# Experts ordered by the picks of eight sequences, and six expert groups taken ahead of the plan

## What is computed

```python
router_probs = softmax(flat_x @ router_w)            # 4096 tokens, 8 experts
topk_w, topk_idx = top_k(router_probs, 2)
topk_w = topk_w / sum(topk_w)
combine = sum(one_hot(topk_idx, 8) * topk_w[..., None], axis=1)
for e in range(8):
    h = gelu(flat_x @ w_fc[e])                       # 256 x 1024
    out = out + combine[:, e:e+1] * (h @ w_proj[e])  # 1024 x 256
```

## Time and profile before

| what | value |
|---|---|
| median of 3 runs | 686.19 us (685.14 to 688.24) |
| the profiled execution | 685.08 us |
| its span in the profile | 682.7 us, mean granted clock 0.961 |
| TensorE matmul busy | 615.7 us (90%) |
| VectorE busy | 490.1 us (72%) |
| GpSimd busy | 404.6 us (59%) |
| ScalarE busy | 397.0 us (58%) |

### The profile page before, as it was taken

The page is one execution under the profiler, slowest core; times in us unless marked ns, Lnnn a source line. Parts: engine busy times, 40 slices in busy tenths (PEclk is TensorE's granted clock), DMA queues, the critical chain, the costliest instruction groups (busy, mean ns, idle before and its releaser), DMA issues. The chain is left out here.

```text
span 682.7 us, 15315 instructions
## 1 busy us (share of the span) xinstructions
PE 615.7 (90%) x4664; PEld 587.4 (86%) x4664; DVE 490.1 (72%) x1162; ACT 397.0 (58%) x694; POOL 404.6 (59%) x298
## 2 busy tenths in 40 slices
PE   2796999999820999999999999999999999999993
PEld 2685888888720999999999999999999999999993
DVE  7663668788777687786768778676877868766661
ACT  3704666776524465656666565666656566656661
POOL 5101121667877567676676667667666766777773
PEclk9996999999965899999999999999999999999997
DMA  8906741232338446523131322313132232312111
GB/s 345 308 2 246 262 162 39 82 110 105 136 110 220 97 142 180 149 57 47 31 63 31 57 37 46 48 31 63 31 56 38 46 48 32 56 24 41 32 25 16
DMA packets 37588, 62.35 MB, mean 91 GB/s; under 512 B 3696, under 2 KB 32944, under 8 KB 36400
## 3 DMA queue, kind: packets, MB, share of 16 engines
q0 software_dynamic: 13296, 18.00, 14.8%
q1 hardware_dynamic: 14816, 34.56, 14.5%
q10 hardware_dynamic: 9440, 9.36, 5.5%
HBM read 37.02 MB, written 24.89 MB: 91 GB/s over the span
## 5 line engine op out<-in xcount | busy, mean ns | idle before, releaser
L625 POOL TENSOR_TENSOR pj_lo<-w_ffn,pj_hi 128x1024 fp32r<-128x1024 f32 x78 | 189.0, 2429 | 101.5 <-ACT pj_hi L685 96.8
L1368 DVE TENSOR_TENSOR fc_lo<-w_ffn,fc_hi 128x1024 fp32r<-128x1024 f32 x78 | 113.4, 1487 | 79.1 <-ACT fc_hi L685 79.1
L614 POOL DMA_INDIRECT out<-y,add_id x71 | 112.7, 1587 | 42.5 <-issue 41.5
L685 ACT ACTIVATE pj_hi<-w_ffn 128x1024 fp32r x78 | 82.6, 1060 | 89.7 <-PE psO L1693 77.0
L685 ACT ACTIVATE fc_hi<-w_ffn 128x1024 fp32r x78 | 79.0, 1053 | 36.5 <-issue 35.9
L1693 PE MATMUL psP<-pj_hi,h_hi 128*128 128x256 f32 x312 | 92.2, 295 | 2.7 <-DVE h_lo L1368 2.7
L1693 PE MATMUL psP<-pj_hi,h_lo 128*128 128x256 f32 x312 | 88.5, 284 | 0.0
L1693 PE MATMUL psP<-pj_lo,h_hi 128*128 128x256 f32 x312 | 88.3, 283 | 0.0
L582 POOL DMA_INDIRECT slots<-rows,slot x64 | 64.1, 1001 | 18.3 <-issue 16.5
L572 POOL TENSOR_TENSOR roots<-ve,power 128x6 f32<-128x6 f32 (+2 forms) x20 | 23.0, 1152 | 86.6 <-DVE ve L1045 85.6
L1693 PE MATMUL psO<-pj_lo,h_hi 128*128 128x256 f32 x256 | 72.6, 283 | 0.0
(11 more groups left out here) (302 smaller groups left out, 1592.0 us busy)
## 6 DMA issues: line engine op xcount, KB each, us to landing
w_ffn<-in_w_ffn SPq DMA_DIRECT2D x8, 2048.0 KB, 7.8
xg<-slots ACTq DMA_DIRECT2D x31, 265.0 KB, 2.9
xc<-in_x_ch SPq DMA_DIRECT2D x4, 1024.0 KB, 8.5
out<-x SPq DMA_DIRECT2D x16, 256.0 KB, 2.2
...
out<-y,add_id POOLq DMA_INDIRECT x71, 3.9
...
```

The lines of the kernel that those rows point to most:

```text
L614: nc.gpsimd.indirect_dma_start(out_d, bass.IndirectOffsetOnAxis(ap=add_id[:, s:s + 1], axis=0), y[:, s, :], None, compute_op=ALU.add).then ...
L625: nc.gpsimd.tensor_tensor(pj_lo[:, 4 * a:4 * a + 4, :], w_ffn[:, bass.ds(e, 1), (2 + a) * DFF:(3 + a) * DFF].rearrange("p a (c d) -> p (a ...
L685: nc.scalar.activation(out, src, ACT.Copy, **kw).then_inc(done, 1)
L1368: v.tensor_tensor(out, whole, upper.bitcast(F32), ALU.subtract).then_inc(done, 1)
```

## The change

- The first eight sequences' counts are made known in slot 12 (`known_sum`, `count_known`, `known_in`), and `order_experts` sorts the experts by them, most picked first. Weights are loaded in that order, so the first load is issued after it, in turn with the stores.
- `first_counts` and `first_rows` (slot 13) lay out six full groups (`AHEAD`) from rows of these eight sequences alone. Their rows are loaded once the scatters of eight sequences have landed (`EARLY` becomes 8), not all of them.
- Attention's loop ends at slot 16; ScalarE, VectorE and TensorE prepare group 0 in slots 14 to 16, and TensorE's `up(0)` begins in slot 16.
- The rest of attention's routing and the plan of the other groups is cut in pieces (`tail_early`, `tail_ending`) put between VectorE's steps of groups 0 to 4. The rest of GpSimd's scatters stands between its steps of groups 0 to 4.
- In these six groups (`relieved`) ScalarE makes the upper part of the hidden layer instead of VectorE (`cast`), and VectorE the first half of the projection's lower part instead of GpSimd.
- Group 6's load waits for all scatters and fill rows. Buffers in SBUF and PSUM are laid out anew. Groups 6 to 29 run in the loop of two.

The diff, cut to its core:

```diff
+KNOWN = 1
+EARLY = sum(BATCHES[KNOWN])
+AHEAD = 6
...
-        def weights_in(eng, e):
-
-            if e:
-                eng.wait_ge(ld_w, 16 * e)
-            eng.dma_start(w_ffn[:, (e + LATE) % E, :], w_ffn_d[e]).then_inc(ld_w, 16)
+        def weights_in(eng, n):
+
+            if n:
+                eng.wait_ge(ld_w, 16 * n)
+            e = eng.value_load(order[0:1, n:n + 1], min_val=0, max_val=E - 1)
+            eng.dma_start(w_ffn[:, (n + LATE) % E, :],
+                          w_ffn_d[bass.ds(e, 1)].rearrange("a p n -> p (a n)")).then_inc(ld_w, 16)
...
+        def relieved(g):
+            return isinstance(g, int) and g < AHEAD
...
+            sp.wait_ge(order_ready, 1)
+            weights_in(sp, 0)
+            for n, b in enumerate(range(EARLY + 3, EARLY + 5)):
+                store(b, stored_next)
+                weights_in(sp, n + 1)
+            for b in range(EARLY + 5, B - 1):
+                store(b, stored_next)
+
+
+            sp.wait_ge(meta_read, 2)
+            sp.wait_ge(xg_t_mm, 1)
+            load_group(sp, 1)
+            weights_in(sp, 3)
+            store(B - 1, stored_last)
+            weights_in(sp, 4)
...
+            pool_slot(B + 1)
+            scatter_some(2)
+            conv_rows_gone(pool)
+            pool.wait_ge(first_ready, 1)
+            for g in range(AHEAD):
+                proj_lower(g, range(1, 2))
+                if g > 0:
+                    add(g - 1)
+                scatter_some(4)
+                assert g < AHEAD - 2 or not left
...
+                if k == B - 2:
+                    act.wait_ge(first_ready, 1)
+                    act.wait_ge(scattered_early, SENT * EARLY)
+                    act.sem_inc(act_passed, 1)
+                    load_group(act, 0)
+                    act.wait_ge(spec_lower, B // 2)
+                    fc_upper(0, 0, range(0, 1))
+                if k == B - 1:
+                    fc_upper(0, 0, range(1, DH))
+                    x_upper(0)
+                if k == B:
+                    act.wait_ge(stored_first, 16 * (STORED_FIRST + 1))
+                    proj_upper(0, 0)
...
+            def cast(g, c):
+
+                act.wait_ge(gelu_done, g * 4 + c + 1)
+                copy(h_hi[:, 2 * c:2 * c + 2, :], hidden_in(g, c), h_hi_ready)
...
+                if relieved(g):
+                    proj_upper(g, 1)
+                    if g == 1:
+                        pick_ratio(len(BATCHES) - 1)
+                    gelu(g, 0)
+                    if g == 0:
+                        act.wait_ge(stored_next, 16 * (B - 1 - STORED_FIRST))
+                    cast(g, 0)
+                    if g_on(g - 1):
+                        outputs(g - 1)
+                    if g == 0:
+                        normalise(B - 2, B + 1, 0, rows[:, 2 * B - 4:2 * B - 2, :], xn2_ready)
+                    gelu(g, 1)
+                    cast(g, 1)
+                    fc_upper(g + 1, 1 - par, range(0, 1))
+                    gelu(g, 2)
+                    cast(g, 2)
+                    fc_upper(g + 1, 1 - par, range(1, DH))
+                    gelu(g, 3)
+                    cast(g, 3)
+                    if g == 0:
+                        normalise(B - 1, B + 2, 0, rows[:, 2 * B - 2:2 * B, :], xn2_ready)
...
+                    if isinstance(g, int) and g + 2 == AHEAD:
+                        slots_there(act)
+                        act.wait_ge(idle_stored, 16)
...
+                if k == B - 1:
+                    alone(spec_upper, B)
+                    fc_lower(0, 0, expert_of(0), range(0, 1))
...
+                if k == sum(BATCHES[KNOWN]) + 4:
+                    order_experts()
+                if k == sum(BATCHES[KNOWN]) + 5:
+                    first_counts()
+                    first_rows()
+                if k == B - 1:
+                    fc_lower(0, 0, expert_of(0), range(1, DH))
+                    slot_meta(0)
+                    conv_rows_gone(dve)
+                    dve.sem_inc(dve_passed, 1)
+                    x_lower(0)
...
+            def tail_early(g):
+
+                if g == 0:
+                    pick(last, 0)
+
+                if g == 1:
+                    weigh(last)
+                if g == 4:
+                    half_groups()
+
+            def tail_ending(g):
+
+                if g == 0:
+                    pick(last, 1)
+                    gap_scale(last)
+                    count_picks(last)
+                    carry_out()
+                if g == 1:
+                    alone(counts_mm, 1)
+                    where_in(last)
+                    find_slots(last)
+                    counts_out()
+                if g == 2:
+                    plan_ends()
+                    plan_rows()
+                if g == 3:
+                    plan_weights()
+                    half_counts()
+
             def dve_group(g, par):
-                if is_half(g):
+                if relieved(g):
+                    proj_lower(g)
+                    hidden(g, 0)
+                    hidden(g, 1)
+                    e = expert_of(g + 1) if g + 1 < AHEAD else None
+                    if e is None:
+                        planned(dve, g + 1)
+                        e = expert_of(g + 1)
+                    fc_lower(g + 1, 1 - par, e, range(0, 1))
+                    slot_meta(g + 1)
+                    tail_early(g)
+                    if g == 0:
+                        alone(stored_next, 16 * (B - 1 - STORED_FIRST))
+                        alone(xn2_ready, 2 * B - 2)
+                    hidden(g, 2)
+                    hidden(g, 3)
+                    x_lower(g + 1)
+                    fc_lower(g + 1, 1 - par, e, range(1, DH))
+                    tail_ending(g)
...
             def pe_slot(k):
                 if on(k):
                     query_keys(k)
                     values(k)
+                if k == B:
+                    up(0, 0, range(0, 1))
                 if on(k - 1):
                     probs_t(k - 1)
+                if k == B:
+                    up(0, 0, range(1, 2))
```

603 lines of the change are left out of this document (366 added, 237 removed).

## The result

| what | before | changed |
|---|---|---|
| median of 4 runs | 685.66 us (684.97 to 688.24) | 695.02 us (693.44 to 695.83) |
| ratio | | 1.0131, 95% interval 1.0109 to 1.0153 |
| span of the profiled execution | 682.7 us | 693.9 us |
| row transposes of group 1 | 231.06 | 214.50 |
| row transposes of group 6 | 291.3 | 305.20 |

The change made the kernel slower by 1.3%. The prediction had 680.6 (669 to 690), so both its sign and its range were wrong. Three stretches tell where the time went. At group 1 the changed kernel is 16.6 us ahead. In five groups it loses 30.5 us against the kernel before (90.7 instead of 60.2), so that at group 6 it is 13.9 behind. From there on it gains: 388.7 us to the end instead of 391.4. That gives 11.2 us, the difference of the spans.

The account below looks back on a forecast made before the run. TensorE was taken to bound the expert groups, idle only at the seam. Of 37.1 us at best, delays left 9.8; less 3 for clock and 1.2 for port, 5.6 us gained: 679.5 profiled, 680.6 median (669 to 690).

Parts of the forecast that it names:

- the best case: Seam between scores' end at 186.07 and group 1's row transposes: 231.06 could become 194.0, saving 37.1 us.
- A: Attention's last slots: added VectorE work and ScalarE's wait for a scatter before group 0's row load; 7.9 us lost.
- Part (1): VectorE's added instructions in attention's last slots: 11 after slot 12 (2.5 us), 25 after slot 13 (5.4 us).
- B: First x_lo, at the end of VectorE's slot 15: TensorE waits for it after scores end; 3.0 us lost.
- Nothing or hidden: Terms put at no cost, among them weights loaded only after the order, early stores and fills, and straight code for six groups.
- R3: Rival: group 6 waits for scatters and fills that end no sooner, nearly all gain waited off; 685 us, chance 0.19.
- Fills end near 245.: Fill rows end near 245 us while group 6 asks at 267, so they cost nothing.
- C: Groups 0 and 1: casts, normalisations and three table loads on ScalarE, a first choice on VectorE; 8.1 us lost.
- E: TensorE's clock falling to 1.2 GHz after the new gaps; 3 us lost, bounds 0 and 7.
- D: Plan pieces on VectorE behind groups 0 to 4, 3.9 us hidden by TensorE's up; 8.0 us lost.
- F: VectorE's plan pieces blocked by GpSimd's subtraction on the shared port; 1.2 us lost, bounds 0 and 12.
- R2: Rival: the shared port costs the full 2.4 us in each of five groups, 12.0 in all; 691 us, chance 0.14.

Follow-up runs that it names:

- fixed_order: ratio_and_regs with experts in their own order and the first five 2 MB weight loads issued before attention; 0.9877 of the kernel before.
- rows_first: Changed kernel with the third 2 MB weight load moved from ahead of group 0's row load to behind group 1's; 1.0023 of the kernel before.
- no_gpsimd_cast: loads_in_turn with VectorE also making the second half of pj_lo in the six groups, GpSimd's 2.40 us subtraction gone; 0.9986 of the kernel before.
- ratio_gpsimd: no_gpsimd_cast with the last batch's ratio made by one GpSimd power instruction instead of ScalarE's exponential between table loads; 0.9931 of the kernel before.
- ratio_and_regs: ratio_gpsimd with ScalarE reading the next group's expert and landing numbers once instead of twice a group; 0.9897 of the kernel before.
- fills_early: Changed kernel with SyncE's eight fills waiting for the tail counts instead of the whole plan; 1.0082 of the kernel before.
- loads_in_turn: Changed kernel with each 2 MB weight load behind a landed row load, fills waiting for counts alone, no scatters left for group 4; 1.0028 of the kernel before.
- half_plan_late: loads_in_turn with the half groups' plan moved from groups 3 and 4 to groups 5 and 28; 1.0172 of the kernel before.
- plan_shifted: ratio_and_regs with half-plan counts moved to group 4, its rows to group 5, and fills behind group 4's rows; 0.9940 of the kernel before.

## Why the prediction was wrong

**What bounds the kernel, and the best case.** Right: the seam was the place, and 37.1 us the most to be had. 16.6 of them were there at group 1.

**A, 7.9 us.** Too small. The softmax of sequence 14 came 14.4 us late (193.69 against 179.33) where 9.1 was worked out, and ScalarE stood 6.0 us instead of 4. 2.2 us of it were there in slot 12 already (the maximum at 165.19 instead of 163.02), before any new work. Most of that looks like luck: a softmax of that slot stands at 164.04 in the kernel before and 166.21 in the changed one, at 164.7 to 165.0 in the three other traces built on the kernel before, and between 164.3 and 166.8 in those built on the changed one. About 0.9 us of it is one small VectorE instruction at 10 us, which took 0.21 in the kernel before, 1.11 here, and either length in the other runs. The scatter that ScalarE waits for was issued at 183.15, and the row load behind it went out 7.8 us later, at 190.94; fixed_order shows 3.5 us with no weights under way. The prediction took 5.0 us for a scatter to land and no weights beside it. (Its own terms give 186.0 for that landing, not 186.3.) Part (1) was right in size: the 25 instructions stand from 175.33 to 180.80, 5.4 us.

**B, 3.0 us.** Right: TensorE waits 2.49 at 205.43. But up(0) began there 6.3 us later than A and B had it (199.1), and took 3.3 us longer: some 1.7 because the first pairs ran at the lower clock (0.56 to 0.63 us instead of 0.40, 3.4 us at a granted clock of 0.50), the rest mostly the attend of the last sequence, which the sum had ahead of it. So group 1's transposes come at 214.5 instead of 204.9.

**"Nothing or hidden", weights.** This is the first of the two steps that failed. The term was put at nothing, since the prediction asked only whether weights come in time. It did not ask what queues behind them: the rows of group 0 took 9.4 us, where the median of all 31 such loads is 3.0, TensorE waited 3.0 us for them, and the scatter and row load of A came late too. These are the larger part of the 9.6 us that group 1 is behind the forecast (rows_first has it 5.6 us sooner, fixed_order 1.6 sooner than its base). R3 had the mechanism, a load's 7.8 us standing ahead of others, but for the scatters of group 6 alone. rows_first prices the row load at 0.6 to 1.1 points. The Trainium skill states the rule ("DMA: Bandwidth & Descriptors", section "Issuing engines are not separate DMA queues": transfers run on the same 16 DMA engines whichever engine issued them), and the two slow row loads agree with it.

**"Fills end near 245."** Wrong as a reading of the code: SP waits for the second count of plan_ready, which comes with the whole plan at 278. It cost little, since the last scatter was later still (S against F).

**C, 8.1 us.** Right: the waits for h_lo of groups 0 and 1 are 2.6, 3.2 and 2.9 us, 8.8 in all. The clock behind them is E's matter.

**D, 8.0 us.** The second step that failed. Up to group 6 the terms, E and F included, gave 79.1 us from group 1; measured were 90.7. Of the 11.6 us of difference some 6 are waits, and some 6 are TensorE's slower work (E). Of the 22.4 us of waits, 13.6 lie behind group 1, where D had 6.5 up to group 6 and 1.5 behind it. D's cover of 3.9 us a group was the error. Behind group 2 it left 1.2 us; TensorE waited 4.66 at 270.33. The piece took 8.1 us there (259.50 to 267.56) instead of 5.0, since one small instruction stood for 3.10 us beside GpSimd's subtraction, and another 0.8 us of register read stands between it and the subtraction of pj. Behind the pieces ScalarE's chain (about 11 us from the end of one down product to x_hi) has no room to give it back. no_gpsimd_cast, ratio_gpsimd and ratio_and_regs take these apart: 0.4, 0.55 and 0.3 points, the last not clear of noise. The remaining 3.8 us are group 6's rows, of which D had 1.5: the release came at 296 and the load stood behind weights once more.

Of the table loads, C had the number and the size right (three, 1.28 us each). The Trainium skill, page "ScalarE: Activation LUTs", section "What ACT_TABLE_LOAD costs", has about 2.7 us for a switch, of which some 1.3 are the load itself, as in the trace, and the rest a drain. In no_gpsimd_cast two loads and the exponential between them take 2.82 us together, from 224.13 to the Gelu at 226.95, so 1.3 a switch with no drain to be seen; the measurement decides.

**E, 3 us (0 to 7).** Too small. Between the transposes of groups 1 and 6 slow matmuls cost some 7.9 us, and up(0) 1.7 more. It was priced as a term of its own, while it goes with the waits: 22.4 us of waits brought some 7.9 with them, and 2.5 us of the two together are luck, as fills_early shows. Its upper end held three falls in full; the windows show the clock below 1 in five of six.

**F, 1.2 us (0 to 12).** The mechanism was right, the place too, and the size too small: taking the subtractions away gave 0.4% though it put 7 us more work on VectorE. That F falls into D's cover was the same mistake as above: two small instructions stood still for 3.1 and 2.4 us. The Trainium skill's rule ("SBUF — State Buffer", section "Who interferes with whom", one engine holds the shared port for a whole instruction) agrees with the rows of loads_in_turn, half_plan_late and plan_shifted: each long instruction ends within 0.1 us of a subtraction of GpSimd.

**What no step had.** The layout's 0.17 us a group, in the changed kernel from group 6 on; by itself it made the kernel before 0.9% faster. "Buffers are laid out anew" was read as costing nothing, and TensorE's pace as fixed. Without it the result would have been some 2.2% slower, if the parts multiply.

**The rivals.** R2 had the sign and part of the mechanism; it wanted 2.4 us in five groups from the port alone. R3 had the wait for group 6. What came was some of both, with the row load and the clock, and they were priced as alternatives when they add up. Group 6 at 305 lies where the prediction said it would be wrong: after 292.
